# A three-layer attention kernel on one core: separate part buffers for batch 1, operands stored in four blocks and fetched in two runs

## The reference

```python
    x = x + _L0_attn_a_ref(_layernorm(x, axis=-1), ...)   # windowed: 16 heads of 8, window of 32, token 0 global
    x = x + _L0_ffn_ref(...)                              # ternary weights
    x = x + _L0_attn_b_ref(...)                           # gated recurrence, forward and backward
    x = x + _L0_ffn_ref(...)
    x = x + _L1_attn_a_ref(...)                           # full attention, 16 heads of 8
    x = x + _L1_ffn_ref(...)                              # top-1 of 8 experts
    x = x + _L1_attn_b_ref(...)                           # full attention
    x = x + _L1_ffn_ref(...)
```

## Time and profile before

| | |
|---|---|
| median of 3 executions | 1089.73 us (1089.5 to 1090.9) |
| the profiled execution: its own time | 1093.83 us |
| its span in the profile | 1092.1 us, mean granted TensorE clock 0.943 |
| PE busy | 997.3 us (91%) |
| DVE busy | 832.2 us (76%) |
| ACT busy | 727.6 us (67%) |
| POOL busy | 165.0 us (15%) |
| chain that ended last, by engine | DVE 54%, PE 34%, issue 5%, DMA 3%, ACT 2% |
| DMA moved | 64.48 MB, mean 59 GB/s |

### The profile page before, as it was taken

The page is one execution under the profiler, slowest core; times in us unless marked ns, Lnnn a source line. Parts: engine busy times, 40 slices in busy tenths (PEclk is TensorE's granted clock), DMA queues, the critical chain, the costliest instruction groups (busy, mean ns, idle before and its releaser), DMA issues.

```text
span 1092.1 us, 32508 instructions
## 1 busy us (share of the span) xinstructions
PE 997.3 (91%) x13437; PEld 459.5 (42%) x13437; DVE 832.2 (76%) x1023; ACT 727.6 (67%) x1469; POOL 165.0 (15%) x438
## 2 busy tenths in 40 slices
PE   6799999779768999999999999999999999999997
PEld 2445545433333344444444444344434444443443
DVE  4545654256755999999979799978879997899932
ACT  3513445347332699999767699957669986697780
POOL 8200101016100000000112210010221001010100
PEclk8789989879887999999999999989999999999999
DMA  3753532100027122310000025300003520010000
GB/s 106 205 181 87 109 90 71 54 1 1 1 80 211 39 68 58 69 35 18 26 10 15 23 71 135 88 12 13 15 21 106 125 64 13 12 37 27 13 28 23
DMA packets 60387, 64.48 MB, mean 59 GB/s; under 512 B 17424, under 2 KB 39184, under 8 KB 60112
## 3 DMA queue, kind: packets, MB, share of 16 engines
q1 hardware_dynamic: 60240, 62.40, 21.6%
HBM read 27.06 MB, written 35.32 MB: 57 GB/s over the span
## 4 chain that ended last, share of the span: by engine, by line
DVE 54%; PE 34%; issue 5%; DMA 3%; ACT 2%; SPq 1%; POOLq 0%; POOL 0%; DVEq 0%; ACTq 0%
DVE nmf L1672 45%; PE wide L691 23%; PE bank L691 11%; DVE xcsq L1443 1%; DVE xp L1443 1%; DMA x<-xT 1%; DVE big L1821 1%; DVE xcsq L1452 1%; ACT scr L1202 1%; DMA KQs<-mw_dram 1%; SPq L446 1%; DVE res L1443 1%; DVE nmt L1611 1%; ACT L1202 0%; DVE big L1443 0%
## 5 line engine op out<-in xcount | busy, mean ns | idle before, releaser
L1672 DVE TENSOR_REDUCE nmf<-wide 128x1 f32<-128x1024 f32 x512 | 590.9, 1217 | 34.5 <-PE wide L691 34.1
L1202 ACT ACTIVATE big<-wide 128x512 f32<-128x512 f32 x683 | 391.3, 601 | 94.1 <-PE wide L691 82.6
L691 PE MATMUL wide<-big,KQs 48*128 48x512 bf16 (+1 forms) x1376 | 354.4, 348 | 3.7 <-DVE nmf L1672 2.1
L691 PE MATMUL bank<-big,V 128*9 128x128 f32 x8192 | 326.2, 278 | 11.9
L691 PEld LDWEIGHTS bank<-big,V 128*9 128x9 f32 x8192 | 177.7, 90 | 236.6 <-ACT big L1202 192.1
L691 PE MATMUL wide<-KQs,big 50*128 50x512 bf16 (+1 forms) x1035 | 270.2, 327 | 0.0
L1202 ACT ACTIVATE big<-bank 128x512 f32<-128x512 f32 (+1 forms) x469 | 231.8, 514 | 49.8 <-PE bank L691 44.5
L691 PE MATMUL bank<-KQs,big 50*128 50x512 bf16 x341 | 132.3, 388 | 0.0
L1202 ACT ACTIVATE scr<-wide 128x380 f32<-128x380 f32 (+3 forms) x128 | 61.3, 486 | 82.8 <-PE wide L691 71.7
L620 POOL CAST nms<-nmf 128x4 bf16<-128x4 f32 x128 | 23.9, 187 | 605.9 <-DVE nmf L1672 605.9
L691 PEld LDWEIGHTS wide<-KQs,big 50*128 50x128 bf16 x1035 | 69.8, 95 | 104.9 <-ACT big L1202 52.9
(11 more groups left out here) (214 smaller groups left out, 813.6 us busy)
## 6 DMA issues: line engine op xcount, KB each, us to landing
o_dram<-big SPq DMA_DIRECT2D x128, 64.0 KB
big<-kf_dram SPq DMA_DIRECT2D x32, 200.0 KB
kf_dram<-scr SPq DMA_DIRECT2D x24, 256.0 KB, 3.7
qf_dram<-scr SPq DMA_DIRECT2D x24, 256.0 KB, 3.9
KQs<-qf_dram SPq DMA_DIRECT2D x32, 192.0 KB
ow_dram<-scr SPq DMA_DIRECT2D x32, 142.5 KB
big<-kw_dram SPq DMA_DIRECT2D x16, 275.0 KB
kw_dram<-scr SPq DMA_DIRECT2D x12, 352.0 KB, 5.9
```

Of the source, the lines that this page charges most:

```text
L691: return nc.tensor.matmul(o, l, r, start=start, stop=stop, **kw)
L1202: return nc.scalar.activation(o, i, f, **kw)
L1672: nc.vector.tensor_reduce(nmf[:, i % 4, c:c + 1], wide[:, k:k + 2, :].rearrange("p g c -> p (g c)"), AX.X, ALU.max, negate=True).then_inc( ...
```

## The change

1. Batch 1 has its own part buffers (`partk`, `partq`, `partf` become lists; batch 1's lie in regions of `big` and `xcsq` that are idle then). ACT's waits for the stores of batch 0 go.
2. Four blocks are stored instead of six (`STORED`: k as 0,0,1,2, q as 2,1,0,0), and each operand is fetched as two runs of 24 rows (`rows_in`, `RUN`): k from blocks 1 to 3 and then 0 to 2, q from blocks 0 to 2 and then 1 to 3. A group is eight DMAs instead of four. The ones go straight into SBUF, by four DMAs of one row each (`ones_rows_in`), before each of the two kinds of attention.
3. Query 0's scores come from the parts: six bf16 products instead of one float32 matmul (`zero_scores`); `kf` goes; DVE takes the first column of the three parts (`zero_heads`).
4. SP's list: batch 1's windowed stores move from ahead of `turned(0)` into units 0 and 1 of the main list, the fetches of groups 4 and 5 from units 2 and 6 to units 4 and 7. In the full attention both groups 0 and 1 are fetched before the stores of batch 1, and `true_x` stands before the projections on DVE.
5. Fillers: 22 become 8 ahead of the windowed attention, 24 become 14 ahead of the full one, and PE starts the latter and the maximums there before it waits for the end of the projections.
6. POOL's constants: half the zeroing of `s0` moves behind the projections; the block of ones is smaller.

The diff, cut to its core:

```diff
-ROW_PARTS = ((2, 1, 0, 1, 0, 0), (0, 1, 2, 0, 1, 0))
+STORED = ((0, 0, 1, 2), (2, 1, 0, 0))
+RUN = ((1, 0), (0, 1))
+PRODUCTS = ((2, 0), (1, 0), (1, 1), (0, 0), (0, 1), (0, 2))
...
+        partk = [blocks(scr, 0, KW), blocks(big, o, KW)]
+        partq = [blocks(scr, 2 * KW, QW), blocks(xcsq, 0, QW)]
...
+        partf = [[blocks(t, 3 * S // 2 * i, S) for i in range(2)] for t in (scr, xcsq)]
...
-        LOADS_W = {2: 4, 6: 5, 10: 6, 14: 7}
+        LOADS_W = {4: 4, 7: 5, 10: 6, 14: 7}
...
+            def ones_rows_in(t):
+                cols = t.shape[1] * t.shape[2] // 64
+                for r in (KR, KR + 1, 64 + KR, 64 + KR + 1):
+                    row = t[r:r + 1, :, :].rearrange("r n c -> r (n c)").rearrange("r (a c) -> r a c", c=cols)
+                    sp.dma_start(row, onesb[:, 0:cols]).then_inc(ones_in, 16)
+
+            def rows_in(dst, r, k, src, signal):
+                for a in range(2):
+                    o = D * RUN[k][a]
+                    sp.dma_start(dst[r + 3 * D * a:r + 3 * D * (a + 1)], src[o:o + 3 * D]).then_inc(signal, 16)
...
-                for b in range(B):
-                    for k in (1, 0):
-                        store(b, k)
-                    if b == 0:
-                        sp.wait_ge(ones_out, 32)
-                        for k in range(2):
-                            sp.wait_ge(partw_out[k], 96)
-                        load_group(0)
-                        load_group(1)
-                for k in range(2):
-                    sp.wait_ge(partw_out[k], 96 * B)
+                for k in (1, 0):
+                    store(0, k)
+                load_group(0)
+                load_group(1)
...
+                    if u < 2:
+                        store(1, 1 - u)
...
+                sp.wait_ge(fp_first, 1)
+                ones_rows_in(kop)
                 for b in range(B):
                     for k in range(2):
                         sp.wait_ge(fp_third, 4 * b + 2 * k + 2)
-                        for j in range(6):
-                            store_full(k, b, j)
+                        for j in range(4):
+                            store_full(k, b, j, partf[b])
...
-                    if b == 0:
...
                         load_group(0)
-                for k in range(2):
-                    sp.wait_ge(part_out[k], 96 * 2)
-                load_group(1)
+                        load_group(1)
...
-                ins = mm(bk(3 + t // 5)[0:H, 0:k * QT].rearrange("p (t k) -> p t k", k=QT),
-                         q0m[:, b, :], cols[:, :, HALF:HALF + QT])
+                    for n, (i, j) in enumerate(PRODUCTS):
+                        cols = partk[b][:, i, t * P:(t + k) * P].rearrange("p (t k) -> p t k", k=P)
+                        ins = mm(o, q0m[:, b, j, :], cols[:, :, HALF:HALF + QT], start=(n == 0), stop=(n == 5))
...
-                keep_busy(2, bk(6))
-                keep_busy(20, bk(7))
+                keep_busy(8, bk(7))
...
             def full_attentions():
-                pe.wait_ge(fp_res, 8)
-                pe.wait_ge(fp_v, NC)
                 pe.wait_ge(x_out, NC)
+                keep_busy(14, bk(7))
...
-                        if b and at == 0:
-                            act.wait_ge(partw_out[int(kind == "q")], 96)
-                        if kind == "k":
-                            o = partk[:, :, at:at + cols]
-                            fn(kf[:, b * KW + at:b * KW + at + cols], src, ACT.Copy)
...
                 if stage == 4:
+                    true_x()
                     project_full(1)
-                    true_x()
```

More of the change, by code:

```diff
@@ L145, in build @@
         denw = sb("denw", [P, B, P])
[L146 to L149, removed]
+        q0f = sb("q0f", [P, B, 3])
+        q0m = sb("q0m", [P, B, 3, H], BF16)
+        s0 = [t[0:H, o - KW:o].rearrange("p (t k) -> p t k", t=WT) for t, o in ((scr, 6496), (xcsq, 2 * N))]
         s0s = sb("s0s", [H, B, 4])
@@ L441, in windowed_attention, with store_full @@
                 batch_in(1)
-            def store_full(k, b, j):
+            def store_full(k, b, j, parts):
                 dst = (qf_dram if k else kf_dram)[j * D:j * D + D, :, S * b:S * b + S].rearrange("d h c -> h d c")
-                sp.dma_start(dst, partf[:, k, ROW_PARTS[k][j], :]).then_inc(part_out[k], 16)
-            def load_full(b, k, odd, p0, p1, group):
-                dst, src, rows = (qop, qf_dram, KR) if k else (kop, kf_dram, KR + 2)
-                r = 64 * odd
-                sp.dma_start(dst[r:r + rows, p0:p1, S * b:S * b + S],
-                             src[:, 2 * p0 + odd:2 * p1:2, S * b:S * b + S]).then_inc(op_in[group], 16)
+                sp.dma_start(dst, parts[k][:, STORED[k][j], :]).then_inc(part_out[k], 16)
             def full_attentions():
@@ L458, in load_group @@
                     for odd in range(2):
-                        for k in range(2):
-                            load_full(b, k, odd, p0, p0 + 2, 2 * g + odd)
+                        for k, (t, dram) in enumerate(((kop, kf_dram), (qop, qf_dram))):
+                            rows_in(t[:, p0:p0 + 2, S * b:S * b + S], 64 * odd, k,
+                                    dram[:, 2 * p0 + odd:2 * p0 + 4:2, S * b:S * b + S], op_in[2 * g + odd])
                 def shift(i):
@@ L519, in full_attentions @@
                         pair(i + 2)
+                    if i == min(n for n in LOADS if LOADS[n] >= GROUPS):
+                        for k in range(2):
+                            sp.wait_ge(part_out[k], 64 * 2)
                     if i in LOADS:
@@ L528, in full_attentions @@
                         if STORE <= o < STORE + 4:
[L529 to L530 removed]
+                            for j in range(2):
+                                store_parts(r, (o - STORE) // 2, (o - STORE) % 2 * 2 + j)
                         if o in LOAD:
@@ L1557, in zero_heads @@
             def zero_heads():
-                dve.wait_ge(part1, QK_W)
+                dve.wait_ge(part3, QK_W)
                 dve.wait_ge(q0_const, 1)
                 for b in range(B):
-                    ins = nc.vector.tensor_scalar(q0m[:, b, :], hmask[:, :], q0f[:, b:b + 1], None, ALU.mult)
+                    ins = nc.vector.tensor_copy(q0f[:, b, :], partq[b][:, 0:3, 0])
+                ins.then_inc(q0_parts, 1)
+                dve.wait_ge(q0_parts, 1)
+                for b in range(B):
+                    for i in range(3):
+                        ins = nc.vector.tensor_scalar(q0m[:, b, i, :], hmask[:, :], q0f[:, b, i:i + 1], None, ALU.mult)
                 ins.then_inc(g0v, 1)
```

135 lines of the change are left out of this document (67 added, 68 removed).

## The result

| | before | after |
|---|---|---|
| median of 20 executions | 1090.14 us (1087.5 to 1095.4) | 1096.49 us (1091.3 to 1101.3) |
| ratio, 95% interval | | 1.0054 (1.0039 to 1.0069) |
| the profiled execution: own time, span, granted clock | 1093.83, 1092.1, 0.943 | 1096.42, 1094.4, 0.936 |

The account below looks back on a forecast made before the run. DVE and full-clock TensorE bound the full attentions; gains lay in the windowed projections and before the full attention. -11.5 + 1.6 + 3.5 - 8.7 = -15.1 us, from 1089.7 to 1074.6; range 1064 to 1084.

Parts of the forecast that it names:

- The clock ahead of the full attention: Maxima ahead of the first full scores: TensorE starts them at 1.2 GHz, costing 2 us in all.
- Rival (a): Half clock through batch 1's projections or when the full maxima begin takes part of the gain: 1080.8 us; chance 0.20.
- The start: Up to the first windowed maximum: waits, copies and fillers go, operands come last; 11.5 us earlier, bounds 7 and 13.
- a wait for operands beyond 48 us: Start, a sign of being wrong: PE waiting for `kw_dram` beyond 48 us; first windowed maximum was forecast near 46.
- Query 0: Its scores before unit 0: bf16 products take 2.7 us instead of 1.93, twice; +1.6 us, bounds 1.2 and 3.5.
- The windowed units: Shifts queue behind group fetches, so PE waits at units 8, 11 and 14; +3.5 us, bounds -5.4 and +10.
- Rival (b): Windowed units: 24-row pieces spread better, fetches get quicker and no shift is late; 1065.7 us; chance 0.22.
- The transition: Before the full attention: ACT's waits go, operands come last; first maximum at 334.6; -8.7 us including slow maxima, bounds -5 and -13.
- Full attentions: Four more issues of 0.33 us per fetch stay hidden, PE waits for no DMA: no change.
- Rival (c): Group fetches: twice the pieces take twice the time, so shifts come 5.7 us later still; +4.4, 1094 us; chance 0.06.
- Rival (d): Waits on stores turn into waits on fetches and late shifts eat the rest: net nothing, occupancy near 10 us; chance 0.05.

Follow-up runs that it names:

- a1: Kernel after, with 46 fillers instead of 14 ahead of the maxima of the first full attention; 1083.55 us, ratio 0.9929 to the kernel before.
- a2: Kernel after, with its 14 fillers placed behind PE's wait for the operands of slot 0; 1085.89 us, ratio 0.9945.
- b1: Kernel before, with 4 fillers instead of 24 ahead of the maxima of the full attention; 1100.86 us, ratio 1.0083.
- j1: Kernel after, with six instead of two fillers behind each of the first four full-attention maxima; 1087.00 us, ratio 0.9968.
- c3: c1 with ACT again waiting for batch 0's stores before writing batch 1's first k or q; 1090.02 us, ratio 0.9999.
- a3: Kernel after, with 24 fillers instead of 8 ahead of the windowed maxima; 1091.76 us, ratio 0.9999.
- c1: Kernel after, with 24 fillers for 8 ahead of the windowed maxima and 46 for 14 ahead of the full ones; 1078.23 us, ratio 0.9898.
- f2: f1 with the half-group fetches moved to units 5 and 6, 8 and 9, 13 and 14, 18 and 19; 1074.63 us, ratio 0.9830.
- f1: c1 with groups 4 to 7 each fetched in two halves, one unit apart; 1075.79 us, ratio 0.9869.
- c2: c1 with the fetches of groups 4 to 7 at units 5, 11, 14 and 20; 1083.15 us, ratio 0.9915.
- a4: Kernel after, with the fetches of groups 4 to 7 at units 5, 8, 14 and 17; 1095.82 us, ratio 1.0041.

## Why the prediction was wrong, point by point

- **The clock ahead of the full attention: the step that failed.** The text said: "The fillers are over 5 us before, so I expect TensorE at 1.2 GHz when the maxima begin; each then costs PE more than DVE's 1.14 us, for 2 us in all." The state was right and its length wrong: the level did not come back with the maxima, for 31 us and on until 374, and the term was 13.1 instead of 2. I took for granted that a busy PE gets its clock back; a1, a2, b1 and j1 show that this mix does not. Rival (a) had the place and the sign, and its size was off in the same way.
- **The start** gave 8.85 of 11.5 us. The removed waits, copies and fillers were right (PE ready at 45.3, computed 45.2; with the waits back, c3's projections end 6.0 us later, for 7.0 forecast). Mis-sized was when the operands land: the k stores were issued from 36.74 instead of 35.2, the fetch from 43.33 instead of 41.3, and half a group took 5.3 us instead of 4.4. So the gain ended where the operands landed, not where PE was ready; a wait for operands beyond 48 us is one of the signs of being wrong that the text had named.
- **Query 0** cost 4.0 us instead of 1.6, for the first one ran at half clock. At full clock it is 0.92 us twice, near the 0.8 predicted. The text had the half clock in its bound of 3.5 and not in the sum: it reckoned 0.5 us of wait ahead of the maxima, and that became 3.3.
- **The windowed units:** waits at 8, 11 and 14 as forecast, 5.6 us in all. That the stretch gave +3.25 for +3.5 is in part luck: it took 224.49 us in the trace before but 221.71 in b1, the same program there, and 225.1 to 225.3 in a2, a3 and j1, 227.74 in the trace after and 231.3 in a1, again one program. Rival (b) was wrong: the 24-row pieces did keep somewhat more of the engines busy, 0.75 from 330 to 335.4 us, where a fetch before had 0.69 (387 to 391) and 0.60 in its tail, but the shifts were late all the same.
- **The transition:** operands landed at 335.41. Relative to the last `xp` that is 26.46 us for 23.57 predicted, the last store having landed after 4.8 us for 3.9 and been issued 0.9 us later, and the fetch having taken 6.6 for 5.7. No wait of ACT on a store, as forecast. Of the 7.88 us won 7.4 are the time of the 24 fillers, which PE no longer runs behind the operands.
- **Full attentions:** PE waited for no DMA after its first slot, and the last stretch is the same within 0.9 us, as forecast.
- **Rival (c)**, the only one with the right sign, was wrong: half a group lands no later in eight pieces than in four (5.1 and 5.3 us), and the measured +2.27 has nothing to do with it. Rival (d) was right that waits on stores turn into waits on fetches (3.3 and 7.3 us), but not by its occupancy of 10 us, and the late shifts were not what ate the gain. The right result needed a rival of its own: that the fillers removed were what the clock of the next stage lived on.
- **Slips in the text** that change little: 57.5 - 45.8 is 11.7 and not 11.5; 325.0 + 3.9 is 328.9 and not 328.6; and the 637 us of the earlier trace rows are the full attentions only up to 1000 us.

The sum, with the measured terms: -8.85 + 3.52 + 3.25 - 7.88 + 13.14 - 0.91 = +2.27. With both clocks kept (c1) the same change gives -1.0% in the runs: 11 us for the 15.1 predicted.

## What to carry to other kernels

Work that shortens a stage may take away what kept TensorE's clock up for the next one. Count fillers from the end of real work to the instant when what PE waits for lands, or put them behind the wait, and read the granted clock of the stage that follows, not only busy time. A short wait can cost far more than its own length: 1.39 us was followed by 20 us at half clock in f2. In a queue shared with long transfers, moving one only moved the wait; cutting it in two looked better, within the noise. And when a part of a change is taken back to price it, fit the fillers to the new waits, or they are in the price, as in c3.

## What the runs showed of the hardware that I had not expected

- A stretch in which PE has no gap or next to none can stay at 1.2 GHz for 31 us (335.4 to 366.3 after; 339.2 to 370 in b1), and the windowed units for 20 us (f2). In these units it came back with the twelve fillers of a pause: after (140.28), f1 (155.61) and f2 (180.5). It can come back without: in c2 it was down from 169.2 to 172.6 us only and rose during unit 25, 5 us ahead of the next pause.
- What a small gap costs varies from one execution to the next. The last stretch, almost the same program in all, took 723.4 to 726.2 us in nine of the fourteen profiled executions and in 727.6 to 733.2 in the other five. In four of these (a1, a4, c1, c3) the clock is down for 7 to 10 us some 184 to 188 us after the first full scores, among the projections of the other layer; in the fifth (j1) and in the nine it is down there for 3.4 us or not at all. The same 12 us of c3 and of f1:

```profile
540.00:552.00 12.00, 11.74 (x96) 7.21 (x92) 5.51 (x7) 4.65 (x10) 2.43 (x5) 0.59 0.03 6
```

```profile
528.40:540.40 12.00, 11.49 (x150) 6.60 (x148) 7.85 (x10) 6.21 (x13) 2.43 (x5) 0.86 0.03 8
```

  What tips it was not tried. It is part of the spread of about 10 us between executions of the kernel after (clock 0.939 at 1091.3 us, 0.926 at 1101.3).
